# A graph network's prologue: spacing increments moved ahead of a TensorE stage, and its matmuls made two tiles wide

## What is computed

```
h = max(layernorm(x), 0)
x = x + hypergraph_conv2(relu(hypergraph_conv1(h)))     # W1, b1, then W2, b2
h = max(layernorm(x), 0)
x = x + edge_mlp_and_node_mlp(h, src, dst, edge_weight)
```

## Time and profile before

| what | us |
|---|---|
| runs (3) | 8141.06, 8156.17, 8164.4 |
| the profiled execution | 8149.92 |
| its span, first to last instruction | 8148.2 |
| the first block | 0 to 163.7 |
| edge network | about 5,500 to 8,044 |

### The profile page before, as it was taken

One profiled execution on the slowest core, in us unless ns is written; L12 is line 12 of the kernel. 1 busy time (PEld: TensorE's weight loads), 2 busy tenths in 40 slices (PEclk: granted clock), 3 DMA queues, 4 the chain that ended last, 5 costly groups with the idle time before them and its releaser, 6 DMA issues. The chain is left out here.

```text
span 8148.2 us, 251180 instructions
## 1 busy us (share of the span) xinstructions
PE 7491.0 (92%) x79908; PEld 7026.0 (86%) x79908; DVE 7075.0 (87%) x15335; ACT 5267.2 (65%) x12972; POOL 3200.4 (39%) x4180
## 2 busy tenths in 40 slices
PE   4899999999999998999888899949999999999998
PEld 3788888888888887999888899938999999999997
DVE  6999999999999995888888888868899999999996
ACT  2888998989898981000477788835666666666664
POOL 1999999999999990000000000001111111111110
PEclk9999999999999999999999999969999999999999
DMA  2677777777777778666799899964333334333434
GB/s 69 138 165 175 167 176 165 176 167 173 169 174 169 172 172 201 191 190 190 199 222 221 207 244 241 241 175 121 114 114 114 113 115 116 115 113 115 116 114 101
DMA packets 1533191, 1309.72 MB, mean 161 GB/s; under 512 B 810544, under 2 KB 1347556, under 8 KB 1531404
## 3 DMA queue, kind: packets, MB, share of 16 engines
q1 hardware_dynamic: 1515918, 1269.86, 63.7%
q0 software_dynamic: 14112, 26.84, 1.2%
q10 hardware_dynamic: 2240, 0.66, 0.1%
HBM read 778.02 MB, written 361.62 MB: 140 GB/s over the span
## 5 line engine op out<-in xcount | busy, mean ns | idle before, releaser
L719 POOL TENSOR_SCALAR OH<-iot,kd 128x102 bf16<-128x102 bf16 x3440 | 2659.4, 793 | 0.0
L2329 POOL DMA_INDIRECT Qx<-tab_q,tidx x294 | 349.1, 1188 | 4511.3 <-DVE skt L2363 2390.3
L1573 ACT ACTIVATE AF<-RG 128x1536 fp32r<-128x1536 uint8 x686 | 1022.8, 1491 | 1192.6 <-DMA RG<-adj 889.9
L1024 ACT ACTIVATE RB<-PS 128x512 uint8<-128x512 f32 x2401 | 1409.7, 601 | 90.7 <-PE PS L884 46.0
L1543 PE MATMUL wp<-AF,XS 128*128 128x256 f32 x9604 | 1215.7, 284 | 143.4 <-issue 84.6
L900 PE MATMUL HP<-T3a,RB 128*128 128x193 bf16 x9604 | 1209.0, 249 | 119.1 <-ACT RB L1024 114.5
L1543 PEld LDWEIGHTS wp<-AF,XS 128*128 128x128 f32 x9604 | 1158.1, 191 | 176.9 <-issue 174.4
L2350 ACT ACTIVATE Z<-Zb 128x512 f32<-128x512 f32 x882 | 556.1, 630 | 978.4 <-DVE Zb L2407 978.2
L900 PEld LDWEIGHTS HP<-T3a,RB 128*128 128x128 fp8e4 x9604 | 864.7, 98 | 203.7 <-issue 149.6
L1639 DVE CAST AF<-RG 128x2048 fp32r<-128x2048 uint8 x686 | 817.5, 1223 | 151.2 <-DMA RG<-adjT 74.8
L2300 PEld LDWEIGHTS p<-eW2s,Y 128*128 128x128 f32 x7056 | 923.2, 191 | 24.0
(11 more groups left out here) (344 smaller groups left out, 14691.2 us busy)
## 6 DMA issues: line engine op xcount, KB each, us to landing
RG<-adjT SPq DMA_DIRECT2D x1372, 224.0 KB, 7.6
sdb<-bk SPq DMA_DIRECT2D x245, 768.0 KB
adj<-RB SPq DMA_DIRECT2D x343, 448.0 KB, 2.9
adjT<-RT SPq DMA_DIRECT2D x686, 224.0 KB, 3.8
RG<-adj SPq DMA_DIRECT2D x686, 224.0 KB, 4.5
sdb<-bk SPq DMA_DIRECT2D x49, 384.0 KB
WR<-wk SPq DMA_DIRECT2D x882, 9.0 KB
tab_p<-Pst SPq DMA_DIRECT2D x25, 512.0 KB, 3.0
```

Source lines behind the costliest of these rows:

```text
L719: ins = e.tensor_scalar(OH[:, g * GT + k, :], iot1[:, 0:KEYS], kd[:, g * GT + k:g * GT + k + 1], None, ALU.is_equal)
L1024: e.activation(RB[n % NSLOT][:, k, :].bitcast(u8).rearrange("p (n x) -> p n x", x=2), bank(u)[:, :].rearrange("p (x n) -> p n x", x=2), AC ...
L1573: e.activation(floats((b + n) % 3, VB, PB), counts(n, VB, PB), ACT.Copy).then_inc(h_ca, 1)
```

## The change

Four edits, all in the first block:

- `spaced(e, SPACE1)` stands ahead of TensorE's work in the block, still with 136 increments.
- TensorE transposes two tiles at once (128x128, both tiles' features down the partitions) and multiplies by `Wd`, a 128x128 matrix with `W1` twice on its diagonal and zeros elsewhere. Per group that is two transposes and two matmuls of 128x128.
- The copy at line 388 reads 128 partitions x 256 columns in place of 64 x 512, and applies `Relu`; VectorE's clip (line 216) is left out, and TensorE waits for the seventh step of the layer norm.
- `Wd` needs two more weight loads (64x64 each) and two clearing writes (64x64 each) on VectorE.

```diff
@@ class Norm, vector
-                link(e.tensor_scalar(to, to, 0.0, None, ALU.max))
+                if clip:
+                    link(e.tensor_scalar(to, to, 0.0, None, ALU.max))
@@ weights
+        Wd = sbt(root, "Wd", [P, 2 * F], fp32)
+            loads.append((Wd[n * F:(n + 1) * F, n * F:(n + 1) * F], W1))
@@ buffers of the prologue
-            lin.buffers(st, "w")
+            ptw, pow_ = ([pst(st, f"{n}w{k}") for k in range(2)] for n in ("pt", "po"))
+            hTw = [sbt(st, f"hTw{k}", [P, 2, P], fp32) for k in range(2)]
@@ ScalarE
-                            e.activation(lin.hT[g % 2][:, :, :].rearrange("p j n -> p (j n)"), lin.pt[g % 2][0:F, :], ACT.Copy).then_inc(lin.copied, 1)
+                            e.activation(hTw[g % 2][:, :, :].rearrange("p j n -> p (j n)"), ptw[g % 2][:, 0:2 * P], ACT.Relu).then_inc(lin.copied, 1)
@@ TensorE
-                    e.wait_ge(norm.steps, 8)
+                    spaced(e, SPACE1)
+                    e.wait_ge(norm.steps, 7)
                     e.wait_ge(s_w, 16 * len(loads))
                     e.wait_ge(s_fill, 3)
-                    lin.tensor(e, 0, X0, nW["W1s"])
-                    spaced(e, SPACE1)
+                    for g in range(NG + 1):
+                        if g < NG:
+                            if g >= 2:
+                                e.wait_ge(lin.copied, g - 1)
+                            for y in range(2):
+                                ins = e.transpose(ptw[g % 2][:, y * P:(y + 1) * P],
+                                                  X0[:, g * GB + 2 * y:g * GB + 2 * y + 2, :].rearrange("p j f -> p (j f)"), idn[:, :])
+                            ins.then_inc(lin.turned, 1)
+                        if g >= 1:
+                            q = g - 1
+                            e.wait_ge(lin.copied, q + 1)
+                            if q >= 2:
+                                e.wait_ge(lin.out, q - 1)
+                            for y in range(2):
+                                ins = e.matmul(pow_[q % 2][:, y * P:(y + 1) * P], lhsT=hTw[q % 2][:, y, :], rhs=Wd[:, :], start=True, stop=True)
+                            ins.then_inc(lin.made, 1)
@@ VectorE
+                    e.memset(Wd[0:F, F:2 * F], 0.0)
+                    e.memset(Wd[F:2 * F, 0:F], 0.0)
-                    norm.vector(e, X0, acc64, X0[:, :, :])
+                    norm.vector(e, X0, acc64, X0[:, :, :], False)
```

More of the change, by code:

```diff
@@ L198, in __init__, with vector @@
                 self.steps, self.root, self.n = sem(f"n_{name}"), sem(f"r_{name}"), 0
-            def vector(self, e, X, sq, to=None):
+            def vector(self, e, X, sq, to=None, clip=True):
                 to = Hn if to is None else to
@@ L374, in turned_sums @@
             def turned_sums(g):
-                return held(lin.po[g % 2][:, 0:GB * F].rearrange("p (j n) -> p j n", n=F), g)
+                return held(pow_[g % 2][:, 0:GB * F].rearrange("p (j n) -> p j n", n=F), g)
             with nc.Block() as block:
```

## The result

The changed kernel takes 8174.69 us (median, 8160.47 to 8192.63), the kernel before 8142.98 (8120.27 to 8164.4), 20 runs each: ratio 1.0038, 95% interval 1.0029 to 1.0046. That is slower by 0.4%, a little more than the 0.3% that can be told from no change. Forecast were 8125 and a range that ends at 8162; the case that came true had 0.07. In the profiled executions the span goes from 8148.2 to 8174.4 us, +26.2.

The account below looks back on a forecast made before the run. VectorE was taken to bound the first block up to group 14, then TensorE's groups, then its increments. Gains 6.9 + 11.0 + 16.4 = 34.3 us, less 3 at back edges, give -31: 8125 from 8156.2, range 8104 to 8162.

Parts of the forecast that it names:

- The clip leaves VectorE: First block: the maximum moves into ScalarE's copy, so VectorE's first long operation starts 3.53 us sooner.
- the first group comes sooner: First block: half the transposes and passes let VectorE's first add come earlier, a gain of 3.4 us.
- TensorE's group gets shorter: First block's tail behind group 14: TensorE needs 1.57 us per group in place of 2.89, a gain of 11.0 us.
- The increments: End of the first block: the 136 increments move into TensorE's wait for the layer norm, a gain of 16.4 us.
- Small additions: First block: two weight loads and two clearing writes are covered by the layer norm; taken as 0 us.
- What a shorter instruction stream does: Edge network's back edge: 300 fewer TensorE instructions shift its fetches; 3 us lost, bounds 11 gained to 68 lost.
- back edges cost more than the prologue gives: Rival, edge network: every turn waits for two fetches in a row, up to 3.6 us; some 8183 us, slower; chance 0.07.
- Back edges take half of it back: Rival, edge network: the fetch's request sets its landing, 20 to 45 us lost; typically 8150, no change; chance 0.24.
- TensorE's fetches are covered: First large stage: GpSimd is the bound there, so TensorE's instruction fetches cost nothing.

Follow-up runs that it names:

- 256 increments: The changed kernel with SPACE1 = 256 in place of 136, 120 increments more: 8089.03 us, ratio 0.9928 to the kernel before.
- 76: The changed kernel with SPACE1 = 76 in place of 136, 60 increments fewer: 8098.48 us (one run).
- 336: The changed kernel with SPACE1 = 336 in place of 136, 200 increments more: 8113.61 us, ratio 0.9963 to the kernel before.
- the first run: The changed kernel with SPACE1 = 180 in place of 136, 44 increments more: 8101.82 us, ratio 0.9948 to the kernel before.
- 216: The changed kernel with SPACE1 = 216 in place of 136, 80 increments more: 8109.85 us (one run).

## Why the prediction was wrong

*The clip leaves VectorE* (3.53) and *the first group comes sooner* (3.4): right in mechanism. The wait ahead of the first add is 0.89 (forecast 0.8). The add of group 14 comes at 115.32 and not 113.95: 5.6 us in place of 6.9. Most of the difference is that the whole layer norm runs 1.2 us later than before, because `X0` lands later (its first operation starts at 23.08 in place of 21.91).

*TensorE's group gets shorter* (11.0): measured 14.2: from group 14's add to the end of the last one were 25.8 us (120.87 to 146.71) and are 11.6 (115.32 to 126.95). The group takes 1.28 us in the first half of the tail and about 0.88 in the second, against 1.57. The row taken as nearest, the first of the earlier trace rows, stands at half clock, and so does the first half of the tail; there six operations follow each other 0.213 us apart and the two pauses of 0.13 us that the sum added are not seen. In the second half, at full clock, TensorE is no longer the bound: it waits for ScalarE's copy (the 0.20 us at 124.81), ScalarE goes from copy to copy and VectorE is busy 5.14 of 5.90 us. The prediction named these two as next, but at 1.1 us a group; that the pace comes near its lower bound of 0.9 for TensorE is chance.

*The increments* (16.4): 16.7. *Small additions* (0): not quite, as far as is known. The landing of `X0` was to be delayed by a hundredth; the layer norm starts at 21.9 to 22.6 us in the four runs without the two more weight loads and clearing writes, and at 22.6 to 23.7 in the ten with them, 0.7 us later on average. Which of them does it was not tried. Sum 36.5 against 34.3, within the bounds.

*What a shorter instruction stream does* is the step that failed: "It seems to wait for that transfer, not for its request; then a request somewhat later costs little. I take 3 us." Measured: 64.5 us, 44.5 of waiting and 20.8 of longer matmuls at a lower clock behind it (by the rows of the stage). The upper bound in the same paragraph, 68, was nearly met, but it was made of waits alone. The inference rested on one fetch behind one busy stretch of the DMA. The runs show that the fetch's start relative to the branch moves with the place of the code, and the wait with it, while the data traffic is the same in all these runs (0.38 to 0.40 of the DMA). So the request sets the time, and not the transfer ahead of it. The rule of the Trainium skill ("Runtime: NRT & Kernel Launch", section "Instruction fetch mechanics"), that fetches come in blocks of 256 and that a taken branch out of the window stalls, gave the sign that the row did not; the runs agree with the 256, two places 260 apart behaving alike. They agree with the stall for the changed kernel (3.5 us), but with 256 increments, where the target is fetched 3 us ahead, the taken branch costs 0.45 us and TensorE doesn't wait.

The outcome is the rival *back edges cost more than the prologue gives*, with its price (3.1 us a turn in it, 2.93 measured) but not its mechanism: there are not two fetches in a row, but one that is asked for behind the branch, and a third of the loss is TensorE's clock afterwards, which no case had. Against it I wrote that "only a narrow band of places does this". Three of the eight places tried stall in full, spread over 40 instructions, and three more lose about 1 us a turn against the best (76, 180 and 336). That sentence set 0.07, and with it a range that ended at 8162. *Back edges take half of it back* had the right mechanism, the request, and for the waits the right price: 1 to 2 us a turn, 20 to 45 us, against 44.5 measured. What it lacked is the clock's 20.8 us, and these turn "no change" into a slower kernel.

With the loop put back near its old place (the first run, turn 103.24) the kernel takes 34.7 us less than the one before (8101.82 against 8136.52; 42 by the ratio 0.9948), near the forecast of 31. So the prologue's part of the forecast held, and the place of the loop decided the rest.

"TensorE's fetches are covered" in the first stage held for this change (turn 117.14) and for most places (branch 0.35 or 0.36 us), but not with 216 and 256.

## What to carry to other kernels

An edit ahead of a long loop that changes the number of TensorE's instructions can be worth more through the loop's place than through itself: here 44 instructions are 60 us of 8150. So read the back edge's branch record of every loop in every profile, compare turns before totals, and if a branch takes clearly more than the loop's best (here 0.35 to 0.45 us), try a few paddings where they lie under a wait (here 120 more, which leave the prologue's end at 126.6 us, for 86 us). A padding that suits one loop can spoil another, as 216 does. A prologue edit should be judged with the loop put back in its place.

## What the runs showed of the hardware

- A back edge whose target must be fetched costs 3.4 to 3.7 us in the branch when the fetch starts 1.0 us behind it, 4.4 when it starts 2.0 us behind (first large stage with 216), 1.3 to 1.7 when it has started 0.6 to 1.1 us before, 0.93 at 1.4 us before, and 0.35 to 0.45 at 3 us or more before. A fetch takes about 1 us, and where the branch waits for it the jump is done 1.4 us behind its end.
- Announcing the edge earlier (17.0 in place of 8.5 us) does not bring the fetch forward.
- An increment of a semaphore in TensorE's queue takes about 0.15 us (136 of them lie between 142.43 and 163.29 us in the kernel before).
- A stall of 2.4 us in an otherwise full stage is followed, in 13 of 22 turns, by 3.41 us at a granted clock of 0.50; stalls of about 1 us (22 of them with 336) by none.
- The faster prologue lowers its own clock. The windows view of the kernel before, then of the changed one:

```profile
60.00:121.00 61.00, 48.37 (x200) 38.39 (x200) 57.11 (x48) 20.66 (x47) 0.00 (x0) 1.00 0.13 55
```

```profile
60.00:115.30 55.30, 24.04 (x100) 18.88 (x100) 54.35 (x46) 16.89 (x47) 0.00 (x0) 0.59 0.14 60
115.30:121.10 5.80, 5.21 (x24) 5.25 (x25) 4.13 (x17) 3.72 (x12) 0.00 (x0) 0.50 0.00 0
121.10:127.00 5.90, 4.07 (x28) 3.29 (x26) 5.14 (x17) 5.02 (x17) 0.00 (x0) 0.95 0.00 0
```

PE, busy 48.37 of 61 us before, is busy 24.04 of 55.3 now, and the granted clock goes from 1.00 to 0.59. The tail begins at half clock, with four groups of 1.28 us where the later ones take about 0.88; by these rows that gives some 1.6 us back (an estimate).
